# Input products of the recurrent experts as three float32r passes, with VectorE splitting and GpSimd masking

## The reference, cut to what matters

```python
def _expert(x_seq, Wi, Wh, b, Wo, bo):
    def step(carry, xt):
        h, c = carry
        gates = xt @ Wi + h @ Wh + b            # xt @ Wi is the input product
        i_, f_, g_, o_ = jnp.split(gates, 4, axis=-1)
        c = jax.nn.sigmoid(f_) * c + jax.nn.sigmoid(i_) * jnp.tanh(g_)
        h = jax.nn.sigmoid(o_) * jnp.tanh(c)
        return ((h, c), h @ Wo + bo)
    ...
top_vals, top_idx = jax.lax.top_k(flat_x @ router_w + router_b, K)      # K = 2
rw = jax.nn.softmax(top_vals, axis=1)
mask = (top_idx.T[:, None, :] == jnp.arange(E)[None, :, None])          # E = 8
expert_x = mask[..., None] * flat_x[None, None]      # a token not routed to e is zero
...                                                  # each expert runs over 4 steps
y = jnp.einsum('ken,nk,keno->no', mask, rw, out)
```

## Time and profile before

| | us |
|---|---|
| median of 3 runs (lowest, highest) | 3300.14 (3294.03, 3301.14) |
| the profiled execution | 3291.55 |
| its span, first to last instruction | 3289.7 |
| TensorE busy in the span | 2633.7 (80%) |
| VectorE busy | 1679.7 (51%) |
| ScalarE busy | 1302.0 (40%) |
| GpSimd busy | 203.6 (6%) |
| mean granted TensorE clock | 0.887 of full speed |

### The profile page before, as it was taken

One profiled execution on the slowest core, in us unless ns is written; L12 is line 12 of the kernel. 1 busy time (PEld: TensorE's weight loads), 2 busy tenths in 40 slices (PEclk: granted clock), 3 DMA queues, 4 the chain that ended last, 5 costly groups with the idle time before them and its releaser, 6 DMA issues. The chain is left out here.

```text
span 3289.7 us, 48321 instructions
## 1 busy us (share of the span) xinstructions
PE 2633.7 (80%) x16714; PEld 1793.8 (55%) x16714; DVE 1679.7 (51%) x3602; ACT 1302.0 (40%) x2735; POOL 203.6 (6%) x240
## 2 busy tenths in 40 slices
PE   5389899995749967694986999999499999963973
PEld 3245555553538866482564566565266666642862
DVE  3356666664321620553154677777377776741213
ACT  2155555553202420252552455554145555531321
POOL 0000000000050031000000000000100000005022
PEclk8589999997769988895996999999699999986986
DMA  2344444442221630000101213121233232202651
GB/s 87 107 137 150 153 146 155 154 151 81 112 87 33 204 98 13 4 1 13 39 2 49 100 70 139 70 89 51 60 87 84 64 80 67 49 9 75 200 166 52
DMA packets 166566, 286.94 MB, mean 87 GB/s; under 512 B 44652, under 2 KB 125924, under 8 KB 162292
## 3 DMA queue, kind: packets, MB, share of 16 engines
q1 hardware_dynamic: 152900, 262.80, 25.3%
q0 software_dynamic: 6144, 12.60, 1.3%
q10 hardware_dynamic: 7360, 9.44, 1.0%
HBM read 167.71 MB, written 79.86 MB: 75 GB/s over the span
## 5 line engine op out<-in xcount | busy, mean ns | idle before, releaser
L2949 ACT ACTIVATE lstm_gate<-lstm_g_ps,lstm_bias 128x373 f32<-128x373 f32 x368 | 209.8, 573 | 250.0 <-PE lstm_g_ps L2910 235.6
L3548 DVE TENSOR_REDUCE caus_nmx<-caus_a_ps 128x4 f32<-128x512 f32 (+5 forms) x352 | 215.6, 640 | 106.3 <-PE caus_a_ps L3364 103.6
L2910 PE MATMUL lstm_g_ps<-lstm_state,lstm_w 128*128 128x373 f32 x640 | 253.8, 478 | 6.7 <-DVE lstm_state L3032 4.1
L932 DVE TENSOR_REDUCE rel_nmax<-rel_s_ps 128x1 f32<-128x746 f32 x192 | 178.8, 931 | 153.5 <-PE rel_s_ps L790 128.8
L896 ACT ACTIVATE rel_probs<-rel_s_ps,rel_nmax 128x746 f32<-128x746 f32 x192 | 169.7, 884 | 217.7 <-DVE rel_nmax L932 124.6
L3499 ACT ACTIVATE caus_probsT<-caus_s_ps 128x512 f32<-128x512 f32 (+4 forms) x352 | 189.3, 558 | 149.2 <-PE caus_s_ps L3383 145.6
L436 PE MATMUL moe_hb<-moe_z_part,moe_w1h 128*128 x576 | 157.6, 351 | 64.5 <-issue 54.9
L2904 PE MATMUL lstm_g_ps<-lstm_xm,lstm_w 128*128 128x373 f32 x512 | 202.3, 477 | 0.0
L3364 PE MATMUL caus_a_ps<-caus_ks,caus_qs 96*128 96x128 f32 (+6 forms) x768 | 180.8, 327 | 10.6 <-DVE caus_nmx L3548 10.4
L3383 PE MATMUL caus_s_ps<-caus_qs,caus_ks 98*128 98x128 f32 (+6 forms) x768 | 186.1, 333 | 0.5 <-ACT caus_probsT L3499 0.4
L2910 PEld LDWEIGHTS lstm_g_ps<-lstm_state,lstm_w 128*128 128x128 f32 x640 | 121.8, 191 | 87.0 <-DVE lstm_state L3032 4.7
(11 more groups left out here) (478 smaller groups left out, 5193.6 us busy)
## 6 DMA issues: line engine op xcount, KB each, us to landing
lstm_row<-gates SPq DMA_DIRECT2D x16, 1536.0 KB, 13.8
moe_w<-in_moe_w SPq DMA_DIRECT2D x38, 578.0 KB
moe_ew<-in_moe_w SPq DMA_DIRECT2D x33, 578.0 KB
caus_qs<-caus_xh SPq DMA_DIRECT2D x128, 93.2 KB, 2.1
caus_ks<-caus_xh SPq DMA_DIRECT2D x128, 93.2 KB, 2.1
lstm_row<-gates SPq DMA_DIRECT2D x8, 1152.0 KB, 7.5
moe_x<-moe_xs SPq DMA_DIRECT2D x71, 128.0 KB
moe_ys<-moe_yo SPq DMA_DIRECT2D x71, 128.0 KB, 1.7
```

The source lines that it names most:

```text
L932: nc.vector.tensor_reduce(nmax[now.slot][:, t:t + 1], s_ps[t % 2][:, 0:L], AX.X, ALU.max, negate=True).then_inc(max_ready, 1)
L2910: mm = nc.tensor.matmul(bank, w[e % 2][:, 4 * P + g * P:4 * P + (g + 1) * P], state[e % 2][k or 0][i][:], start=False, stop=True)
L2949: nc.scalar.activation(gate[x % 3][g][:], g_ps[n % RING][:, 0:HALF], ACT.Tanh if g == 2 else ACT.Sigmoid, bias=b[:, e, g:g + 1]).then_inc( ...
L3548: nc.vector.tensor_reduce(nmx[0:rows, slot, heads[0]:heads[-1] + 1, t:t + 1], heads_of(bank[0:rows, :], heads, k1 - k0), AX.X, ALU.max, ne ...
```

## The change

The input product of each gate becomes three float32r passes. Weights and input are each split into a part with the low 12 bits cut off and the rest; the passes are high x high, high x low, low x high. VectorE splits the 512 input columns of an expert's weights in two halves of 256 (`split_weights`), and `zT` once, in eight pieces of 374 columns (`split_z`). For steps 1 and 2, GpSimd multiplies both parts with the gate row, into two pairs of tiles instead of four tiles. `split_weights(e + 1)` stands at the start of VectorE's iteration for item (e, 2, 0, 0). The tile `gT` is gone: its rows are loaded in four DMAs into the row buffers of expert 1, whose load therefore waits for the eight products that read them.

```diff
@@ -2759,6 +2759,9 @@
 
+XM_BUFS = 2
+
+
 def recurrent_items():
@@ -2788,8 +2791,9 @@
         bo = a.sb("bo", [2 * E2, P])
-        gT = a.sb("gT", [2 * E2, B * LP])
-        xm = [a.sb(f"xm{i}", [P, HALF]) for i in range(4)]
+        wi = [[a.sb(f"wi{i}_{j}", [P, 4 * P], F32R) for j in range(2)] for i in range(2)]
+        z_parts = [a.sb(f"z_part{j}", [P, NCH * (HALF + 1)], F32R) for j in range(2)]
+        xm = [[a.sb(f"xm{i}_{j}", [P, HALF + 1], F32R) for j in range(2)] for i in range(XM_BUFS)]
         gate = [[a.sb(f"gate{i}_{g}", [P, HALF]) for g in range(4)] for i in range(3)]
@@ -2797,17 +2801,17 @@
         tc = [a.sb(f"tc{i}", [P, HALF]) for i in range(2)]
-        tmp = [a.sb(f"tmp{i}", [P, HALF]) for i in range(2)]
+        tmp = [a.sb(f"tmp{i}", [P, HALF + i]) for i in range(2)]
         g_ps = [a.ps(f"g_ps{i}", [P, BANK]) for i in range(RING)]
...
                  "xm_ready", "g_full", "g_read", "c_ready", "tc_ready", "h_ready", "v_ready", "st_done", "hw_ready", "o_full", "y_done",
-                 "chain")
+                 "chain", "w_high_done", "w_split", "z_high_done", "z_split")
         (rows_in, b_full, b_added, squashed, start_chain, start_ready, bias_full, bias_ready,
          xm_ready, g_full, g_read, c_ready, tc_ready, h_ready, v_ready, st_done, hw_ready, o_full, y_done,
-         chain) = (a.sem(n) for n in names)
+         chain, w_high_done, w_split, z_high_done, z_split) = (a.sem(n) for n in names)
         block = ctx.enter_context(nc.Block())
@@ -2851,6 +2855,17 @@
 
+        def row_wide(e, r, s, i):
+            at = (s - SLOT_STEPS[r][0]) * LP + i * HALF
+            return rows[e % 2][r][:, at:at + HALF + 1]
+
+        def gates_rows(b):
+            r = b // 3
+            return rows[1][r][0:2 * E2, (b - 3 * r) * LP:(b - 3 * r + 1) * LP]
+
+        def z_cols(s, i):
+            return slice((2 * s + i) * (HALF + 1), (2 * s + i + 1) * (HALF + 1))
+
         def h_cols(s, i):
@@ -2858,8 +2873,11 @@
             sp.dma_start(bo[:], io["lstm_bo"]).then_inc(rows_in, 16)
-            sp.dma_start(gT[:], gates_d[2 * E2:4 * E2, :]).then_inc(rows_in, 16)
+            for b in range(B):
+                sp.dma_start(gates_rows(b), gates_d[2 * E2:4 * E2, b * LP:(b + 1) * LP]).then_inc(rows_in, 16)
             for e in range(E2):
+                if e == 1:
+                    sp.wait_ge(b_full, NCH)
                 if e >= 2:
@@ -2873,11 +2891,11 @@
 
-            pe.wait_ge(rows_in, 48)
+            pe.wait_ge(rows_in, 32 + B * 16)
             for c, (b, half) in enumerate(CHUNKS):
...
                     pe.wait_ge(b_added, c - 1)
-                nc.tensor.matmul(o_ps[c % 2][:, 0:HALF], bo[:], gT[:, cols(b, half)], start=True, stop=True).then_inc(b_full, 1)
+                nc.tensor.matmul(o_ps[c % 2][:, 0:HALF], bo[:], gates_rows(b)[:, half * HALF:half * HALF + HALF], start=True, stop=True).then_inc(b_full, 1)
             pe.wait_ge(b_added, NCH)
@@ -2892,16 +2910,18 @@
                 e, s, k, i = ITEMS[x]
-                z = zT[:, LEAD + s * LP + i * HALF:LEAD + s * LP + i * HALF + HALF]
                 if k is not None:
-                    pe.wait_ge(xm_ready, mask_at[x] + 1)
-                    z = xm[mask_at[x] % 4][:]
+                    pe.wait_ge(xm_ready, 2 * mask_at[x] + 2)
+                    z = [part[:] for part in xm[mask_at[x] % XM_BUFS]]
+                else:
+                    pe.wait_ge(z_split, 2 * s + i + 1)
+                    z = [part[:, z_cols(s, i)] for part in z_parts]
                 for y, g in enumerate(gates_of(x)):
...
                         pe.wait_ge(g_read, n - RING + 1)
-                    mm = nc.tensor.matmul(bank, w[e % 2][:, g * P:(g + 1) * P], z, start=True, stop=(s == 0))
+                    mm = three_passes(nc, g_ps[n % RING][:, 0:HALF + 1], [part[:, g * P:(g + 1) * P] for part in wi[e % 2]], z, True, s == 0)
                     if s > 0:
@@ -2924,13 +2944,14 @@
                         start_bias(ITEMS[x][0])
+                        pe.wait_ge(w_split, 2 * ITEMS[x][0] + 2)
                     gates(x)
...
         def _(act):
-            act.wait_ge(rows_in, 48)
+            act.wait_ge(rows_in, 32 + B * 16)
             for n, (g, kind) in enumerate(((0, ACT.Sigmoid), (2, ACT.Tanh), (3, ACT.Sigmoid))):
@@ -2962,6 +2983,20 @@
                     squash(x - 1)
+
+        @block.gpsimd
+        def _(pool):
+            for n, x in enumerate(masked):
+                e, s, k, i = ITEMS[x]
+                if n % 8 == 0:
+                    weights_in(pool, e)
+                if e == 0:
+                    pool.wait_ge(z_split, 2 * s + i + 1)
+                if n >= XM_BUFS:
+                    pool.wait_ge(g_full, first_gate[masked[n - XM_BUFS] + 1])
+                for j in range(2):
+                    nc.gpsimd.tensor_tensor(xm[n % XM_BUFS][j][:], z_parts[j][:, z_cols(s, i)].bitcast(F32),
+                                            row_wide(e, k, s, i), ALU.mult).then_inc(xm_ready, 1)
 
@@ -3022,10 +3057,10 @@
                     dve.wait_ge(st_done, x + 1)
-                    nc.vector.tensor_tensor(tmp[1][:], state[e % 2][0][i][:], row(e, 2, s, i), ALU.mult)
+                    nc.vector.tensor_tensor(tmp[1][:, 0:HALF], state[e % 2][0][i][:], row(e, 2, s, i), ALU.mult)
                     links.link(weigh(x, h[:], row(e, 3, s, i)))
                     out = wstate[out_at[x] % 2][:]
-                    nc.vector.tensor_tensor(out, out, tmp[1][:], ALU.add).then_inc(hw_ready, 1)
+                    nc.vector.tensor_tensor(out, out, tmp[1][:, 0:HALF], ALU.add).then_inc(hw_ready, 1)
                     if s == 2:
@@ -3045,19 +3080,37 @@
 
-            def mask(x):
-                e, s, k, i = ITEMS[x]
-                n = mask_at[x]
-                if n % 8 == 0:
-                    weights_in(dve, e)
-                if n >= 4:
-                    dve.wait_ge(g_full, first_gate[masked[n - 4] + 1])
-                nc.vector.tensor_tensor(xm[n % 4][:], zT[:, LEAD + s * LP + i * HALF:LEAD + s * LP + i * HALF + HALF],
-                                        row(e, k, s, i), ALU.mult).then_inc(xm_ready, 1)
+            def split_weights(e):
+                weights_in(dve, e)
+                if e >= 2:
+                    dve.wait_ge(g_full, first_gate[at[e - 2, STEPS - 1, None, 1] + 1])
+                for q in range(2):
+                    n, at_q = 2 * e + q + 1, slice(q * 2 * P, (q + 1) * 2 * P)
+                    split2(nc, dve, w[e % 2][:, at_q], tmp[1][:, 0:2 * P], wi[e % 2][0][:, at_q], wi[e % 2][1][:, at_q],
+                           w_high_done, n).then_inc(w_split, 1)
+                    dve.wait_ge(w_split, n)
+
+            def split_z(s, i):
+                n = 2 * s + i
+                split2(nc, dve, zT[:, LEAD + s * LP + i * HALF:LEAD + s * LP + i * HALF + HALF + 1], tmp[1][:],
+                       z_parts[0][:, z_cols(s, i)], z_parts[1][:, z_cols(s, i)], z_high_done, n + 1).then_inc(z_split, 1)
+                dve.wait_ge(z_split, n + 1)
+
+            split_z(0, 0)
+            split_weights(0)
+            split_z(0, 1)
+            def tmp_read(x):
+                earlier = len([y for y in outputs if y <= x - 2])
+                if earlier:
+                    dve.wait_ge(hw_ready, earlier)
 
             for x in range(N + 4):
-                if x + 2 in mask_at:
-                    mask(x + 2)
+                if x < 2 * STEPS - 2:
+                    tmp_read(x)
+                    split_z(1 + x // 2, x % 2)
+                if x < N and ITEMS[x][1] == 2 and ITEMS[x][2] == 0 and ITEMS[x][3] == 0 and ITEMS[x][0] + 1 < E2:
+                    tmp_read(x)
+                    split_weights(ITEMS[x][0] + 1)
                 if x < N:
```

## The result

The changed kernel takes 3368.28 us (median of 4 runs, 3366.06 to 3371.39) against 3300.64 (4 runs, 3294.03 to 3304.27): a ratio of 1.0208, 95% interval 1.0189 to 1.0227, so 67.6 us slower. The profiled execution took 3370.19 us, its span is 3368.3 us and its mean granted clock 0.872.

What follows compares the result with a forecast made beforehand. TensorE was taken to set the pace. Passes -42.0, stall +78.6, clock +12, start +1.5 and GpSimd +3 gave +53.1 us, so 3353 us against the median, range 3318 to 3388.

Steps and rivals of the forecast that it cites:

- Sign, place and mechanism: Slower (chance 0.89): VectorE waits for the load at split_weights(e+1), so TensorE stands for the weighted state, six times.
- The passes: Input products in the recurrent stage: float32r triples save 0.114 us on each of 368 products, -42.0 us.
- The stall: TensorE stands 13.1 us for the weighted state behind VectorE's wait for the load, experts 2 to 7: +78.6 us.
- T: End of VectorE's addition for the last output of expert e-1, which triggers the load of expert e+1.
- The clock: TensorE's clock drops after each of six stalls, 1.7 to 3 us lost each time: +12 us (0 to +18).
- Start: Expert 0: splits before the first gate, three more small DMAs, z pieces ahead of masks: +1.5 us (-1 to +6).
- GpSimd beside VectorE: GpSimd's masks, about 1.0 us each, hold up a VectorE product before each trigger: +3 us (0 to +35).
- rival C: GpSimd and VectorE shut each other out, sixteen operations of 1.0 us an expert: 32 us more, 3385; chance 0.15.
- The sum: Whole kernel: -42.0 + 78.6 + 12 + 1.5 + 3 = +53.1 us.
- The estimate from the copies: GpSimd's masks: 2.4 ns a column from its copies, so about 1.0 us for 374 columns.

Runs made afterwards that it cites:

- wait_alone: The kernel before, plus only VectorE's wait for the whole load of expert e+1 at item (e, 2, 0, 0): ratio 1.0208 to the kernel before.
- own_sem: The changed kernel with the weights counted on a semaphore of their own, each reader waiting for what it reads: ratio 0.9935 to the kernel before.
- own_pool_memset: own_sem with GpSimd writing a constant into the mask tiles instead of the product, masking left out: ratio 0.9867 to the kernel before.
- after_memset: The changed kernel with GpSimd writing a constant into the mask tiles instead of the product, masking left out: ratio 1.0174 to the kernel before.
- own_masks_dve: own_sem with GpSimd's two mask products given to VectorE, GpSimd idle: ratio 0.9935 to the kernel before.

## Why the prediction was right, and where a term was off

**Sign, place and mechanism: shown.** The predicted time was 3353 (3318 to 3388), the measured one is 3368. wait_alone gives such a loss by the wait alone, own_sem takes the wait from 17 us to 4 and turns the sign.

**The passes.** 0.114 us a product was predicted; a gate of two products went from 1.254 to 1.14. The 55.5 us period of own_pool_memset, against 60.4 - 5.2 = 55.2, shows that the 5.2 us a period are there to be had.

**The stall.** 13.1 us each was predicted, 14.1 measured: 84.7 us instead of 78.6. By its steps, with T as in the prediction: TensorE stops at about T+10.1 (T+10.9 predicted), VectorE goes on at T+17.05 (T+18.1), and the weighted state is done at T+24.2 (T+24.0). The landing was earlier than I took from the earlier trace rows. The splits and the chain behind it were longer, 7.1 us instead of 5.9, and the splits beside GpSimd's masks account for all of that: the first pair of operations took 1.5 us more than the second. It repeats six times whole (14.05 to 14.24), as followed. Part of the closeness is luck: after_memset has 12.1, so 13.1 was too long for the wait alone, and the masks, which the term did not hold, added 2.

**The clock.** 4.4 us at the lower clock behind each stall held about 2.3 us of full-clock work (an output product, two triples, a state product), 2.2 us lost each time: 13 us, 12 predicted. That the clock would fall at the start as well was not in the prediction (next term).

**Start: mis-sized.** I had +1.5 (-1 to +6). The 68 input products ahead of the trigger for expert 2 should have saved 7.7 us, and the first trigger came 4.6 later: 12.3 us. after_memset brings back 11.3 of them: it is GpSimd's masks, not the loads or z's splits. In expert 0 TensorE waits directly for the chain through VectorE (VectorE, 1820 to 1850 us, first splits of z alone, then beside masks):

```profile
1820.17 0.36 DVE L427 CAST lstm_z_part<-lstm_tmp 128x374 fp32r<-128x374 f32 x1
...
1831.70 1.01 DVE L427 CAST lstm_z_part<-lstm_tmp 128x374 fp32r<-128x374 f32 x1
...
1842.45 0.84 DVE L3028 SCALAR_TENSOR_TENSOR lstm_cell<-lstm_cell,lstm_start,lstm_gate 128x373 f32<-128x373 f32 x1 [4.47 <-issue]
1843.21 1.32 DVE L3031 TENSOR_TENSOR lstm_tmp<-lstm_gate,lstm_gate 128x373 f32<-128x373 f32 x1
```

TensorE stands 8.7 us there for VectorE, 3.4 in after_memset. Behind two of these waits the clock fell too (TensorE; products of the second line's kind last 0.79 us at the full clock):

```profile
1835.82 1.05 PE L2930 MATMUL lstm_g_ps<-lstm_state,lstm_w 128*128 128x373 f32 x2 [4.50 <-DVE lstm_state L3055]
...
1837.60 1.45 PE L2930 MATMUL lstm_g_ps<-lstm_state,lstm_w 128*128 128x373 f32 x2
...
1874.83 1.61 PE L2940 MATMUL lstm_o_ps<-lstm_wstate,lstm_w 128*128 128x373 f32 x2 [3.12 <-DVE lstm_wstate L3063]
```

The granted clock reads 0.50 from 1836.5 to 1839.5 and until 1880.5 behind the second wait; from 1822 on it never leaves 1.00 in after_memset before its first trigger. About 9 us of work at half the clock lost an estimated 4.6 us; with the 5.3 us of waits that is 9.9 of the 11.3.

**GpSimd beside VectorE: right in kind, put in the wrong place.** I took +3 us, and gave 0.15 to rival C, by which the two exclude each other. Beside a mask 0.54 us becomes 1.33, and a pair of masks 2.2 us instead of 1.93. The long product ends 0.4 us behind the pair, which fits taking turns; that the two merely slow each other is not ruled out. But C priced it at 16 us an expert and had VectorE become the bound; it costs VectorE 6.2 us (48.4 against 42.2 in after_memset), and only instructions that meet a mask are longer. So the cost of C is 2.0 us a period and 11.3 at the start, in the stage 21 us where I took 3, and VectorE never became the bound. The Trainium skill (page SBUF — State Buffer, Who interferes with whom) has this exclusion as a rule; the trace agrees in kind, for GpSimd's products.

**The sum** by what was measured: -42.0 + 84.7 + 13 + 12.3 = 68.0, and 69.3 in the stage. GpSimd has no term of its own in it: its 2.0 a period are in the stall, its 11.3 in the start. Where: +4.6 up to the first trigger, 5 x 11.5 = 57.4 in the periods, +7.3 behind the last trigger (109.5 against 102.2).

**Where the gain went.** The passes are worth 1.3% (own_pool_memset). The shared count costs 2.7% (1.0208 against 0.9935). GpSimd's masks cost 0.7% with the wait gone (0.9935 against 0.9867), half of the passes' gain; they do not relieve VectorE: its busy time rises by 8.1 us an expert (50.02 against 41.90), more than by making the sixteen products itself (48.9 in own_masks_dve). That fits own_masks_dve timing the same.

**Open.** Whether more pairs of mask tiles would help was not tried. Nor was an earlier trigger of the load. What in a copy makes it gentle to VectorE, its one input or its shorter time, was only seen, not separated.

## What to carry to other kernels

Before a wait is put into an in-order queue, date the event it waits for from what triggers it, and compare that with how far the bounding engine gets without anything behind the wait; an average slack of 16 us in 60 did not cover one absence of 17 us. Count a transfer on a semaphore of its own where one consumer needs only that transfer: here this one edit was worth 2.7%. Work with two SBUF inputs that is moved from VectorE to GpSimd is not free for VectorE, so compare VectorE's busy time with and without it before counting it as relief.

## What the hardware showed that I had not expected

- A GpSimd product of 374 columns is 1.0 us (pairs of 1.93 to 1.95); beside VectorE's products pairs are 2.2 to 2.5, and the longest single one is 1.4. The estimate from the copies was right.
- A VectorE product that meets one takes 1.33 us instead of 0.54, and the first two operations of a split of 256 columns 0.95 to 1.11 instead of 0.29; beside GpSimd's constant fills (about 410 ns) the product stays at 543 ns, while those two operations go to 0.5; beside its copies (600 ns) the product is 588 ns in the mean.
- Behind a wait of 3.1 us at the start the granted clock was 0.50 for 5.9 us of TensorE's work; the prediction had looked only at the six long ones.
- The same kernel took 3155 us on one chip and 3307 on another, 5% apart, while the first stretch of this stage took 115.3 us on the first of them and 115.2 on the chip of the kernel before's trace (3301 us). No changed kernel ran on two chips, so how well a ratio carries over was not measured.
